# The carry of an attention-pooling stage enters by a matmul instead of on VectorE

## The reference

```python
x = x + L0(x)   # du = zX*lap_x + zY*lap_y + zR*y*(1-y), reflecting borders
x = x + L1(x)   # attn = tanh(x W1 + b1); scores = attn v
                # p = softmax(where(mask, scores[None, :], -1e30)); pooled = p x / cnt[..., None]
x = x + L2(x)   # x W[subject]^T + b[subject]
x = x + L3(x)   # z = relu(x Wd + bd); y = x + z Wu + bu; layernorm(y) * g + b
```

## Time and profile before

| | us |
|---|---|
| median of 3 runs (lowest, highest) | 719.86 (719.62, 722.68) |
| span of the profiled execution, first to last instruction | 717.1 |
| what the median has beside that span | 2.8 |
| PE busy | 576.8 (80%) |
| DVE busy | 556.4 (78%) |
| POOL busy | 399.2 (56%) |
| ACT busy | 323.1 (45%) |
| mean granted TensorE clock | 0.952 of full |

### The profile page before, as it was taken

How to read it: one execution, slowest core, us unless ns; L and a number is a source line. 1 busy time by engine, 2 the same in 40 slices (tenths; PEclk the granted TensorE clock), 3 DMA queues, 4 the chain that set the end, 5 groups by cost and what they waited for, 6 DMA issues and landing times.

```text
span 717.1 us, 10165 instructions
## 1 busy us (share of the span) xinstructions
PE 576.8 (80%) x2928; PEld 456.4 (64%) x2928; DVE 556.4 (78%) x1149; ACT 323.1 (45%) x545; POOL 399.2 (56%) x260
## 2 busy tenths in 40 slices
PE   0247678979788887969879798888979797799994
PEld 0126555868567765758648685677747686498773
DVE  5565777899959997599958899499987989567542
ACT  0343445434643555335644356254553446444331
POOL 5342652469817685259734588066864587237443
PEclk9999879999999998999989899999999999999998
DMA  5471058004750159002580037500581035101012
GB/s 191 164 240 52 0 177 270 11 16 146 239 174 1 59 187 301 28 15 102 195 260 0 15 135 250 173 0 36 198 268 70 15 132 179 71 1 59 16 74 88
DMA packets 53494, 82.61 MB, mean 115 GB/s; under 512 B 9888, under 2 KB 14496, under 8 KB 53456
## 3 DMA queue, kind: packets, MB, share of 16 engines
q1 hardware_dynamic: 44240, 65.42, 28.4%
q10 hardware_dynamic: 9216, 16.78, 6.2%
HBM read 65.41 MB, written 16.78 MB: 115 GB/s over the span
## 4 chain that ended last, share of the span: by engine, by line
DVE 34%; PE 30%; issue 17%; POOL 12%; ACT 4%; DMA 1%; SPq 1%; DVEq 0%; POOLq 0%; ACTq 0%
PE y L539 8%; POOL x2l L478 6%; PE front_ps L562 5%; DVE x2f L1184 4%; DVE xd L1051 4%; PE front_ps L637 3%; DVE xu L1043 3%; POOL xu L435 3%; DVE pn L1138 3%; PE front_ps L585 3%; PE front_ps L539 2%; DVE wn L1067 2%; DVE zl L1191 2%; DVE mask L1034 2%; PE front_ps L551 2%
## 5 line engine op out<-in xcount | busy, mean ns | idle before, releaser
L460 POOL TENSOR_TENSOR rstd<-ve,minus_half 128x1 f32<-128x1 f32 x64 | 41.5, 652 | 149.1 <-DVE ve L1208 148.9
L478 POOL TENSOR_TENSOR x2l<-x2f,x2h 128x1024 fp32r<-128x1024 f32 x32 | 95.4, 2990 | 51.1 <-DVE x2f L1184 41.4
L539 PE MATMUL y<-wth,x2h 128*128 128x512 f32 x256 | 100.7, 393 | 7.6 <-DVE wtl L1150 7.6
L435 POOL TENSOR_TENSOR xu<-xu,xd 128x1024 f32<-128x1024 f32 x32 | 82.1, 2565 | 41.6 <-DMA xd<-in_x 40.5
L468 POOL TENSOR_TENSOR o_sb<-o_sb,x 128x512 f32<-128x512 f32 x64 | 91.6, 1445 | 18.5 <-ACT o_sb L866 13.8
L539 PE MATMUL y<-wth,x2l 128*128 128x512 f32 x256 | 100.8, 394 | 0.0
L539 PE MATMUL y<-wtl,x2h 128*128 128x512 f32 x256 | 100.4, 392 | 0.0
L637 PE MATMUL front_ps<-th_pt,x 128*128 128x129 f32 x512 | 75.4, 303 | 26.5 <-DVE x2f L1184 26.3
L551 PE MATMUL front_ps<-ident,x 128*128 128x128 f32 x256 | 38.2, 304 | 70.1 <-DVE x L1058 70.1
L637 PEld LDWEIGHTS front_ps<-th_pt,x 128*128 128x128 f32 x512 | 72.3, 216 | 31.9 <-DVE x2f L1184 28.6
L443 POOL TENSOR_TENSOR xd<-xn 128x1024 f32<-128x1024 f32 x32 | 66.8, 2087 | 34.6 <-ACT xn L756 31.2
(11 more groups left out here) (120 smaller groups left out, 1216.5 us busy)
## 6 DMA issues: line engine op xcount, KB each, us to landing
xn<-in_x SPq DMA_DIRECT2D x32, 512.0 KB
out<-o_sb ACTq DMA_DIRECT2D x64, 256.0 KB, 2.0
xd<-in_x SPq DMA_DIRECT2D x24, 512.0 KB
xu<-in_x SPq DMA_DIRECT2D x24, 512.0 KB
wn<-in_L_cond_weight SPq DMA_DIRECT2D x8, 1024.0 KB, 5.7
xu<-in_x SPq DMA_DIRECT2D x8, 256.0 KB
xd<-in_x SPq DMA_DIRECT2D x8, 256.0 KB
wd<-in_L_cond_down_w SPq DMA_DIRECT2D x8, 256.0 KB, 5.7
```

Of the source, the lines that this page charges most:

```text
L435: pool.tensor_tensor(xu[:, sl, :, :], xu[:, sl, :, :], xd[:, sl, :, :], ALU.add).then_inc(pool_b, 1)
L478: pool.tensor_tensor(x2l[q][:, k, :], x2f[:, k % 2, :], x2h[q][:, k, :].bitcast(F32), ALU.subtract).then_inc(x2l_ready, 1)
L539: ins = mm(dst, lhs, rhs, start=first and q == 0, stop=last and q == len(parts) - 1, skip_group_check=True)
```

## The change

Alpha is laid out block-diagonally. `alm` holds for each block j a 128x96 piece in which only columns j, 32+j and 64+j are not zero (the stride of 97 puts them there); its transpose, `ka`, has for block j 128 columns in which only rows j, 32+j and 64+j are not zero. `ka` is split: rows 0 to 63 rounded, rows 64 to 95 the rest (`rest_alpha`, DVE, 32 partitions by 1024). The carries of a slice go the same way: `carry_sums` writes them three times (`cc`), PE transposes them into the free end of bank 2 (`carry_rows`), ACT rounds 96x128 (`round_carry`), DVE puts the rest into rows 32 to 63 (`rest_carry`), and three fp32r matmuls of 260, 390 and 390 columns with 96 rows add alpha times carry to the pooled blocks in PSUM (`carry_in`). `round_x2` and `rest_x2` then read PSUM directly, each in two parts (group 2: 256 columns; groups 0 and 1: 768 columns), and `rest_x2` moves from POOL to DVE. `x2f`, `alb` and `add_carry` are gone; a buffer `zf` of its own holds what used part of `x2f`. The programs of PE, ACT and DVE are written in a new order.

```diff
@@ PE @@
             def pool_blocks(n, k, groups):
                 for g in groups:
                     j0, j1 = GROUPS[g]
-                    last = [NG * u + GROUP_ORDER.index(v) for u in range(k) for v in range(NG)
-                            if GROUP_BANK[u % 2][v] == GROUP_BANK[k % 2][g]]
-                    if last:
-                        pe.wait_ge(x2s, KD * NG * n + max(last) + 1)
-                    elif k == 0 and g < 2:
+                    bank = GROUP_BANK[k % 2][g]
+                    if g == 2 and k > 0:
+                        pe.wait_ge(x2l_ready, 2 * (KD * n + k - 1) + 1)
+                    elif g < 2 and k > 1:
+                        pe.wait_ge(x2l_ready, 2 * (KD * n + k - 1))
+                    elif g < 2 and k == 0:
                         pe.wait_ge(pt_ready, 2 * n + g + 1)
                     else:
-                        pe.wait_ge(alb_ready, n + 1)
+                        pe.wait_ge(ka_ready, n + 1)
...
+            def carry_rows(n, k):
+                pe.wait_ge(cc_made, KD * n + k + 1)
+                mm(C_PS, cc[:, k, :], ident[:, :], is_transpose=True, start=False, stop=True,
+                   skip_group_check=True).then_inc(ct_ps, 1)
+
+            def carry_in(n, k):
+                pe.wait_ge(ct_ready, KD * n + k + 1)
+                for g in GROUP_ORDER:
+                    j0, j1 = GROUPS[g]
+                    ins = mm(front_ps[:, GROUP_BANK[k % 2][g], 0:(j1 - j0) * BW], ct[0:KROWS, k % 2, :],
+                             ka[0:KROWS, j0:j1, :], start=False, stop=True, skip_group_check=True)
+                    if g != 0:
+                        ins.then_inc(x2_ps, 1)
@@ ACT @@
+            def round_carry(n, k):
+                act.wait_ge(ct_ps, KD * n + k + 1)
+                copy(ct[0:KROWS, k % 2, :], C_PS).then_inc(ct_h, 1)
...
             def round_x2(n, q, k):
-                act.wait_ge(x2s, NG * (KD * n + k + 1))
-                copy(x2h[q][:, k, :], x2f[:, k % 2, :]).then_inc(x2h_ready, 1)
+                for part in range(2):
+                    act.wait_ge(x2_ps, 2 * (KD * n + k) + part + 1)
+                    copy(x2_part(x2h[q], k, part), x2_sum(k, part)).then_inc(x2h_ready, 1)
@@ DVE @@
+            def rest_alpha(n):
+                dve.wait_ge(ka_h, n + 1)
+                low = ka[2 * CP:KROWS, :, 0:P]
+                dve.tensor_tensor(low, pair_b[2 * CP:KROWS, :].rearrange("p (j l) -> p j l", l=P),
+                                  low.bitcast(F32), ALU.subtract).then_inc(ka_ready, 1)
+
+            def rest_carry(n, k):
+                dve.wait_ge(ct_h, KD * n + k + 1)
+                low = ct[CP:2 * CP, k % 2, :]
+                dve.tensor_tensor(low, front_ps[CP:2 * CP, 2, 512 - P:512], low.bitcast(F32),
+                                  ALU.subtract).then_inc(ct_ready, 1)
+
+            def rest_x2(n, q, k):
+                for part in range(2):
+                    dve.wait_ge(x2h_ready, 2 * (KD * n + k) + part + 1)
+                    dve.tensor_tensor(x2_part(x2l[q], k, part), x2_sum(k, part),
+                                      x2_part(x2h[q], k, part).bitcast(F32),
+                                      ALU.subtract).then_inc(x2l_ready, 1)
...
                 if m is not None:
                     take_scalars(m)
+                if n is not None:
+                    rest_alpha(n)
                 if b is not None:
                     moments(b, 3)
```

More of the change, by code:

```diff
@@ L271, in before, with x2_sum, x2_part @@
             return t - ring if t >= ring else max(u for u in range(NJ) if u % ring == t % ring) - NJ
+        def x2_sum(k, part):
+            if part == 0:
+                return front_ps[:, 2, 0:2 * BW].rearrange("p (j c) -> p j c", c=BW)[:, :, 0:P]
+            first = GROUP_BANK[k % 2][0]
+            return front_ps[:, first:first + 2, 0:3 * BW].rearrange("p g (j c) -> p g j c", c=BW)[:, :, :, 0:P]
+        def x2_part(a, k, part):
+            if part == 0:
+                return a[:, k, 6 * P:].rearrange("p (j l) -> p j l", l=P)
+            return a[:, k, 0:6 * P].rearrange("p (g j l) -> p g j l", g=2, l=P)
         def half(h):
@@ L698, in program @@
                     pool_blocks(n, 1, (0, 1))
-                    pool_blocks(n, 1, (2,))
-                    pool_blocks(n, 2, (0, 1))
+                    carry_rows(n, 0)
                 if b is not None:
@@ L703, in program @@
                 if n is not None:
-                    pool_blocks(n, 2, (2,))
+                    carry_in(n, 0)
                 if b is not None:
@@ L707, in program @@
                 if n is not None:
-                    pool_blocks(n, 3, (0, 1))
-                    pool_blocks(n, 3, (2,))
+                    pool_blocks(n, 1, (2,))
+                    pool_blocks(n, 2, (0, 1))
+                    carry_rows(n, 1)
+                if b is not None:
+                    adapter_up(b, 1 - q, 5)
+                if n is not None:
+                    carry_in(n, 1)
                 if b is not None:
                     linear(b, 1 - q, 6)
+                if n is not None:
+                    pool_blocks(n, 2, (2,))
+                    pool_blocks(n, 3, (0, 1))
+                    carry_rows(n, 2)
+                if b is not None:
+                    adapter_up(b, 1 - q, 6)
+                if n is not None:
+                    carry_in(n, 2)
+                if b is not None:
                     linear(b, 1 - q, 7)
-                    adapter_up(b, 1 - q, 5)
-                    adapter_up(b, 1 - q, 6)
+                if n is not None:
+                    pool_blocks(n, 3, (2,))
+                    carry_rows(n, 3)
+                if b is not None:
                     adapter_up(b, 1 - q, 7)
+                if n is not None:
+                    carry_in(n, 3)
                 if n is not None:
@@ L901, in program @@
                     scale(b, 2)
+                    keep_x3(b, 5)
+                if n is not None:
+                    round_carry(n, 1)
+                if b is not None:
+                    scale(b, 3)
+                    store(b, 1)
                 if n is not None:
@@ L913, in program @@
                 if b is not None:
[L914 to L915 removed]
+                    keep_x3(b, 7)
+                if n is not None:
+                    round_carry(n, 3)
+                if b is not None:
                     store(b, 3)
@@ L1246, in program @@
                 if n is not None:
-                    add_carry(n, 0, 2)
-                    add_carry(n, 0, 0)
-                    add_carry(n, 0, 1)
-                    carry_products(n, 1)
-                    carry_sums(n, 1)
-                    add_carry(n, 1, 2)
-                    add_carry(n, 1, 0)
+                    rest_carry(n, 0)
                 if b is not None:
@@ L1256, in program @@
                 if n is not None:
-                    carry_products(n, 2)
-                    add_carry(n, 1, 1)
-                    carry_sums(n, 2)
+                    rest_x2(n, q, 0)
                 if b is not None:
@@ L1262, in program @@
                 if n is not None:
-                    add_carry(n, 2, 2)
-                if m is not None:
-                    times_x(m, 0)
+                    carry_products(n, 1)
+                    carry_sums(n, 1)
                 if b is not None:
```

156 lines of the change are left out of this document (80 added, 76 removed).

## The result

The changed kernel takes **773.63 us** (median of 4 runs, 770.91 to 778.73) against 720.31 (4 runs, 719.62 to 722.68) on the same chip: ratio 1.069, 95% interval 1.063 to 1.076. 765 was predicted, with 746 to 782 as the range. The profiled execution is the slowest of the four, 778.73 us with a span of 776.5; that of before was 719.9 with 717.1, so the two traces differ by 59.4 us and the medians by 53.3.

A forecast was written before the change was run, and what follows sets the result against it. No engine is full; PE, DVE and POOL tie at the first half's end, so added PE work costs in full. 6 x 6.6 + 2 + 3.5 = 45 us on a 717.1 span gives 762; median 765 us, range 746 to 782.

The forecast's parts named there:

- the moved wait: Slice 0's last two pooled blocks wait for `rest_alpha` behind `take_scalars`; PE stands 6.4 us instead of 4.17, +2.2 per pass.
- The masks stay long: DVE's last two mask steps, 4.48 us beside POOL, don't shorten, because POOL's L0 sums beside them stay.
- rival 2: DVE freed of POOL: masks shorten, `rest_alpha` ends before 395.65, PE loses no 4.17 us; 698 us in all, chance 0.04.
- carry_in: Three added fp32r matmuls on PE cost 0.47 us per slice; with four transposes 2.4 us per pass, bounds 2.4 and 5.3.
- Rival 3: Every round trip of the carry chain shows: each slice loses 1.5 us more, 801 us in all, chance 0.08.
- First half of the pass: 2.2 + 2.4 + 0.8 + 0.1 = 5.5 us later at PE's instruction at 426.28; bounds 3.3 and 8.4.
- The second half: `diffuse(m, 0)` 10 us later delays load, reflect, `adapter_relu` and last `diffuse`; +7.0 per pass, 6.6 after the clock term.
- Rival 1: The second half swallows part of the shift: only 3 us of a pass remain, 743 us in all, chance 0.12.
- PE's 3.65 us of idle time ahead of it: PE's idle time ahead of the pass's last eight transposes shrinks, and part of its half clock with it: -0.4 us.
- n = 0 and the start: Without b the moved wait is free but the chain uncovered, about +2 us; added setup memsets cost 0.
- the last stretch: Pass n = 7, without masks and with PE always busy: 2.4 + 0.8 + 0.3 = 3.5 us.
- Taking one of them off gains next to nothing: PE, DVE and POOL arrive together at about 426.3; freeing one gains next to nothing, more PE work costs in full.

The follow-up runs named there:

- masks late: `take_scalars` moved behind `carry_sums(n, 0)` on DVE: changed kernel, with `rest_alpha` also right behind `moments(b, 2)`, 721.27 us, ratio 0.995; kernel before, 698.08 us, ratio 0.963.
- moved wait alone: Kernel before plus a 1.2 us DVE reduction behind `take_scalars` that the last two pooled blocks of slice 0 wait for: 737.89 us, ratio 1.020.
- reflect late: Changed kernel with `reflect(m, 2)` moved behind `round_w(n, 1)` in ScalarE's queue: 766.67 us, ratio 1.057 to the kernel before.

## Why the prediction was right, and where its sum was off

The ratios of four kernels split the 6.9% of the change. The masks' early place costs 1.069 - 0.995 = 7.5% in the changed kernel and 1.000 - 0.963 = 3.7% in the one before: 3.8 points, 27 us, of the change come from the masks' place and go with it. With the masks late, the change costs 0.995 - 0.963 = 3.1 points, 23 us. The forecast had 13 us for the moved wait and 32 for the rest. The run with the moved wait alone measured 14, so 39 of the 53 are the rest, and 13 of these go too when the masks move: a cost of the masks for which the forecast had no term of its own.

- **The moved wait** was right to 0.1 us: 6.33 in the trace for 6.4, six times, and 14 us in the run that had nothing else. That moving `rest_alpha` gave 22 us and moving the masks 54 says that the wait was only the first cost of the masks. They also held the sums (23.5 us of waits at `carry_rows` with `rest_alpha` early, 6.9 with the masks late), and they were over three times as long where they stood. How much of the rest is the clock is not measured.
- **The masks stay long** was right, and rival 2's condition failed as argued: 4.42 us without POOL's `x2l` in the changed kernel, 4.45 to 4.49 in the one before. They shorten where the L0 steps aren't beside them. Rival 2 was wrong of the change but described a gain that was there to be had in the order.
- **carry_in** was right: 0.49 us a slice for 0.47, and 1.96 us a pass when doubled. Four slices in eight batches are 15.7 us, most of the 23 that are left with the masks late. The rest: 0.83 us of wait at `carry_rows(3)` (0.8 foretold), the transposes, and a longer wait for `zh` (15.3 us in all against 4.8), less the waits of the old kernel that go. Rival 3, every round trip showing, is refuted: in the full passes none but `carry_rows(3)` shows a wait at the carry.
- **First half of the pass**: 5.5 foretold for the instruction at 426.28, 4.5 measured at it and at the first W transposes of n = 4. (The forecast's upper bound of 8.4 is 2.9 a pass above its 5.5, 17 us for six; it wrote 2.5 and 15.)
- **The second half** came in the predicted order and nearly at the predicted times. By the pass's own time, `diffuse(m, 0)` started 8.8 us later for 10, the reflect step at 436.6 for 437.5, `add_around(m, 2)` at 441.3 for 442.2, and the last diffuse ended at 457.6 for 458.0; the pass grew by 7.0 for 6.6. Rival 1 is refuted by the length of all six passes, none under 5.5. That ScalarE's queue is one link of this chain is shown by the run with reflect late. That the early place of `diffuse(m, 0)` would have helped in the changed kernel itself wasn't tried.
- **The step that failed in size** is "PE's 3.65 us of idle time ahead of it [...] gets shorter, and part of its half clock with it: -0.4". It did not: 3.69 us, and the eight transposes behind it took 1.74 to 1.97 us in all six full passes, against three of six in the trace of before. And the late load opened a second hole ahead of it, 1.8 to 3.6 us at `zh`, that I had followed for its time but not for the clock. In n = 1 and n = 5, where the second half had run at full clock before, it now ran at 0.86 and 0.89, and these passes grew by 12.8 and 11.2 us where 6.6 was foretold; that is 10.8 us of the 14.4 by which the traces differ more than the forecast's 45. With reflect late the hole at `zh` closes, and the time falls by 9 us. That the hole lowers the clock is shown by the rows of n = 1, where the W transposes right behind 3.62 us ran at half clock. For the last x1 transposes it is argued only: they ran at half clock behind 3.7 us in n = 1 of the kernel before with the masks late as well, where the hole at `zh` is 0.8 us at most, and at full clock behind 3.65 us in n = 5 of the kernel before. So part of the two dear passes may be chance of this one trace; the medians differ by 6 us less than the traces.
- **n = 0 and the start** cost 5.4 us instead of 2, where every hand-over of the chain is uncovered (four waits for `ct`, 4.5 us), and the last stretch 4.9 instead of 3.5.
- **"Taking one of them off gains next to nothing"** of the tie at the end of the first half: POOL's `x2l` off gave 8 us, so it was worth about 1 us a batch. Whether the changed kernel has that gain inside its sum was not measured.

The rows of GpSimd and VectorE above show small steps that end with a large GpSimd instruction, one after another. The Trainium skill, "SBUF — State Buffer", section on the two separate sides, says that the port pair the two engines share is an exclusive lock: whichever starts first holds it for its whole instruction, and the other is blocked; it names VectorE steps with two SBUF inputs or in a two-port mode. The trace agrees, with ends 0.03 to 0.23 us behind GpSimd's where GpSimd began first, and a GpSimd step 1.00 us longer where VectorE did. (That the copy and the TENSOR_SCALAR, with one SBUF input, run in a two-port mode is shown by no run here.) It explains why my forecast's page, which speaks of contention only, did not point at the order: with a lock, two mask steps can cost two GpSimd instructions whatever their size. I had read that the masks were slow, not what they waited for.

## What to carry to other kernels

Before a step is put behind others in a queue, look at what those others do to it and what is beside them: here the masks needed to be neither early nor long, and one move of them was worth more (26 us before, 54 after) than anything the change touched. When a change delays a load, price the holes that it opens on PE and the clock behind them, in those passes too that had run at full clock. And measure an operation's price pass by pass, where its engine has no idle time; doubled, the same matmuls seemed to cost 5 us in one queue and 25 in another, and only the passes in which nothing else had changed showed their 2 us.

## What the runs showed of the hardware

- Small VectorE steps took as long as the GpSimd instruction beside them: two steps of 128x200 4.42 us beside GpSimd steps of 2.36 and 1.89, and 0.89 in its gap; a copy of 128x7 1.50 us beside one of 1.89 that had begun 0.42 us earlier.
- Taking `x2l` off POOL did nothing for them: 4.48 us with it, 4.42 without it in the changed kernel and 4.45 to 4.49 in the one before, since other GpSimd instructions lie beside them. With one of those two moved away by a stall they took 2.87.
- A GpSimd step of 1.89 us took 2.89 when a VectorE step of 1.28 had begun 0.14 us before it.
- A matmul of 2 columns with 96 rows held PE for 0.09 us, one of 260 to 390 columns for 0.16: the narrow one costs more than half of the wide one.
- A VectorE step over 32 partitions of 1024 columns took 1.22 us, as one over 128 does.
- With 96 more matmuls in the program, PE stood 3.2 to 3.5 us ahead of the same instruction in two passes (n = 3 and n = 5 in both such kernels), released by nothing that the profile shows.
